# The scan of a two-block transformer: four units of the recurrence side by side in TensorE's array, token rows moved by DMA through scratch memory

## The reference, cut to what matters

```python
inv_n = 2.0 / (MB * Dh)
def step(W, kv):
    kc, vc = kv
    z = jnp.einsum('bhsd,bhde->bhse', kc, W)
    grad = jnp.einsum('bhsd,bhse->bhde', kc, (z - vc) * inv_n)
    return (W - LR * grad, z)
_, zs = lax.scan(step, W0, (k_c, v_c))
```

## Time and profile before

| | us |
|---|---|
| median of three runs | 1100.81 (1100.41 to 1100.90) |
| the profiled execution | 1098.78 |
| its span in the trace | 1097.0 |

### The profile page before, as it was taken

One profiled execution on the slowest core, in us unless ns is written; L12 is line 12 of the kernel. 1 busy time (PEld: TensorE's weight loads), 2 busy tenths in 40 slices (PEclk: granted clock), 3 DMA queues, 4 the chain that ended last, 5 costly groups with the idle time before them and its releaser, 6 DMA issues. The chain is left out here.

```text
span 1097.0 us, 15610 instructions
## 1 busy us (share of the span) xinstructions
PE 1019.1 (93%) x5736; PEld 850.5 (78%) x5736; DVE 733.8 (67%) x1657; ACT 380.9 (35%) x731; POOL 227.2 (21%) x284
## 2 busy tenths in 40 slices
PE   6899999999999999998699999888999887999997
PEld 5688888888888888887588888667777775877775
DVE  7766667666666676666569866577878775466456
ACT  4334333333434333333133222044455433421220
POOL 2222222222222221222110011132222224111011
PEclk9999999999999999999999999999999998999999
DMA  9300000000000000000130000030000000000000
GB/s 302 110 1 1 1 1 1 1 1 1 1 1 1 1 1 1 1 1 16 33 100 1 1 1 1 0 98 0 0 0 0 1 2 1 1 15 15 10 20 19
DMA packets 19058, 20.91 MB, mean 19 GB/s; under 512 B 4905, under 2 KB 14898, under 8 KB 18994
## 3 DMA queue, kind: packets, MB, share of 16 engines
q1 hardware_dynamic: 18994, 20.05, 5.6%
HBM read 17.95 MB, written 2.10 MB: 18 GB/s over the span
## 5 line engine op out<-in xcount | busy, mean ns | idle before, releaser
L393 POOL TENSOR_TENSOR rope_sum<-rope_cos,rope_sin 128x512 f32<-128x512 f32 x80 | 115.0, 1437 | 257.0 <-DVE rope_sin L514 257.0
L429 ACT ACTIVATE rope_exp<-rope_sum 128x512 f32<-128x512 f32 x80 | 50.5, 631 | 205.7 <-POOL rope_sum L393 205.6
L783 PE MATMUL proj<-wo_sb,attn_out_t 128*128 128x256 f32 x512 | 113.2, 379 | 0.7 <-issue 0.7
L783 PEld LDWEIGHTS proj<-wo_sb,attn_out_t 128*128 128x128 f32 x512 | 96.1, 190 | 13.4 <-issue 0.9
L732 PE MATMUL num<-v_ones,score_masked 128*128 128x129 f32 x512 | 100.2, 278 | 5.9 <-DVE score_masked L572 5.9
L1754 DVE SCALAR_TENSOR_TENSOR m_acc<-m_expert,gates,m_acc 128x256 f32<-128x256 f32 x128 | 61.9, 484 | 58.6 <-PE m_expert L1833 52.1
L733 PE MATMUL num<-state,q_t 128*128 128x129 f32 x512 | 99.9, 277 | 0.0
L732 PEld LDWEIGHTS num<-v_ones,score_masked 128*128 128x128 f32 x512 | 83.0, 193 | 13.4 <-DVE score_masked L572 8.0
L511 DVE TENSOR_TENSOR rope_cos<-proj,cos_sb 128x512 f32<-128x512 f32 x80 | 55.3, 691 | 52.6 <-PE proj L686 52.6
L1554 PE MATMUL g_ps<-t_u,k_rows 128*128 128x128 f32 x512 | 72.7, 284 | 17.2 <-DVE t_u L1403 16.4
L1554 PEld LDWEIGHTS g_ps<-t_u,k_rows 128*128 128x128 f32 x512 | 63.4, 191 | 31.0 <-DVE t_u L1403 27.8
(11 more groups left out here) (205 smaller groups left out, 1993.4 us busy)
## 6 DMA issues: line engine op xcount, KB each, us to landing
a_stage<-in_wqkv SPq DMA_DIRECT2D x6, 512.0 KB, 5.4
wo_sb<-in_wo SPq DMA_DIRECT2D x1, 2048.0 KB, 10.1
a_stage<-in_wgu SPq DMA_DIRECT2D x4, 512.0 KB, 9.2
out<-x_sb SPq DMA_DIRECT2D x16, 128.0 KB, 1.7
x_sb<-in_x SPq DMA_DIRECT2D x2, 768.0 KB, 11.5
f_wmod<-in_wmod SPq DMA_DIRECT2D x1, 1536.0 KB, 9.0
w_sb<-in_w SPq DMA_DIRECT2D x1, 1280.0 KB
a_wmod<-in_wmod SPq DMA_DIRECT2D x1, 1024.0 KB, 6.5
```

The lines of the kernel that those rows point to most:

```text
L393: pool.tensor_tensor(y[:, parity], t1[:, parity], t2[:, parity], ALU.add).then_inc(s["y_done"], 1)
L783: mm = pe.matmul(proj[:, b, 0:D], o_t[:, i, :], wo[:, i, :], start=(i == 0), stop=(i == H - 1))
```

## The change

**The scan's layout.** The four units share the array. For z each unit takes a window of 32 columns of k transposed (`k_turned`, of which 16 are of the minibatch) as weights, and writes to 32 partitions of its own of one bank: four matmuls, 32x128. For g each unit has 16 rows on partitions 32 j to 32 j + 15 of `kv_rows` and `u_rows` as weights and moving rows, and a PSUM bank of its own. u is one operation of 128x128 for all units, w one of 128x512. There is one chain in place of one for each batch.

**The rows.** k and v leave the tile layout (a token on a partition) by a DMA to scratch in device memory and come back in row layout, `kv_rows`; u goes the other way, and POOL then makes z as v - u (`keep_z`). All these DMAs are issued by SP.

**The rest.** `k_diag` and `k_rows` are gone, with ACT's work on them and their semaphores. The high part of h is made by ACT, the low part by POOL. Turning, normalising and writing out z happens one tile later (`c - 2` for `out_rows`). The loop over tiles is written out. In the mixture, the gates are padded with zeros from 9 to 128 columns, and b2 to 128 rows.

The diff, cut to its core:

```diff
+            UP = P // U
             xn, zn = self.t_xn, sb("t_zn", [P, B, D])
             h = sb("t_h", [P, B, KD, P])
...
-            k_diag = sb("k_diag", [P, B, KD, NMB * STEP])
-            k_rows = sb("k_rows", [P, B, NMB, D])
-            u = sb("t_u", [P, B, D])
-            w = sb("t_w", [P, B, KD, P])
+            kv = sb("t_kv", [P, 2, B, KD, 2, P])
+            k_t = sb("k_turned", [P, 2, U * P + MB])
+            kv_r, u_r = sb("kv_rows", [P, 2, NMB, 2, P]), sb("u_rows", [P, 2, NMB, P])
+            u_tok = sb("t_u", [P, B, D])
...
+            g_ps = ps("g_ps", [P, U, 512])
+            kv_dram = nc.dram_tensor("kv_scratch", (2, B, P, KD * 2 * P), F32, kind="Internal").ap()
...
-            def walk(engine, step):
-
-
-                step(0, False, True, True)
-                with nc.Fori(1, NC - 2, engines=(engine.engine,), hint_back_edge=True) as c:
-                    step(c, True, True, True)
...
+                def kv_rows(c, b):
+                    q = c % 2
+                    sp.wait_ge(kr_done, nth(b, c + 1))
+                    sp.wait_ge(v_kept, nth(b, c + 1))
+                    sp.dma_start(kv_dram[q, b], kv[:, q, b].rearrange("p k u e -> p (k u e)")).then_inc(kv_out[b], 16)
+                    if c >= 2:
+                        sp.wait_ge(g_full, 1 + (c - 1) * NMB)
+                        sp.wait_ge(u_done, (c - 1) * NMB)
+                    sp.wait_ge(kv_out[b], 16 * (c + 1))
+                    for k in range(KD):
+                        src = kv_dram[q, b].rearrange("(n s) (k d) -> k s n d", n=NMB, k=KD)[k]
+                        sp.dma_start(kv_r[unit(b, k), q].rearrange("s n u e -> s n (u e)"), src).then_inc(kv_in[b], 16)
+
+                def u_rows_out(c):
+                    q = c % 2
+                    sp.wait_ge(u_done, (c + 1) * NMB)
+                    for b in range(B):
+                        for k in range(KD):
+                            dst = u_dram[q, b].rearrange("(n s) (k d) -> k s n d", n=NMB, k=KD)[k]
+                            sp.dma_start(dst, u_r[unit(b, k), q]).then_inc(u_out[b], 16)
+                    for b in range(B):
+                        if c:
+                            sp.wait_ge(z_kept, nth(b, c))
+                        sp.wait_ge(u_out[b], 16 * KD * (c + 1))
+                        sp.dma_start(u_tok[:, b], u_dram[q, b]).then_inc(u_in[b], 16)
+
+                sp.wait_ge(zeroed, 1)
+                for b in range(B):
+                    kv_rows(0, b)
                 w2, b1, b2, gw = self.moe_small
...
+                pool.memset(kv_r[:], 0.0).then_inc(zeroed, 1)
+                pool.memset(k_t[:, :, U * P:U * P + MB], 0.0).then_inc(zeroed, 1)
+
+                def low(c, b):
+                    pool.wait_ge(hi_done, nth(b, c + 1))
+                    pool.tensor_tensor(h_lo[:, b], h[:, b], h_hi[:, b].bitcast(F32), ALU.subtract).then_inc(hl_done, 1)
+
+                def keep_z(c, b):
+                    pool.wait_ge(u_in[b], 16 * (c + 1))
+                    if c:
+                        pool.wait_ge(zn_done, nth(b, c))
...
-                def spread(c, b, j, waited=True):
-
-                    if waited:
-                        act.wait_ge(g_full, nth(b, c * NMB + (j - NMB + 2)))
-                    act.activation(k_rows[:, b, j], kr[:, b], ACT.Copy, scale=rows_of[:, j:j + 1]
-                                   ).then_inc(k_rows_done, 1)
...
+                def high(c, b):
+                    act.wait_ge(h_done, nth(b, c + 1))
+                    if c:
+                        act.wait_ge(proj_full, nth(b, c))
+                    act.activation(h_hi[:, b], h[:, b], ACT.Copy).then_inc(hi_done, 1)
...
+                def residual(c, n):
+                    i = c * NMB + n
+                    dve.wait_ge(z_full, i + 1)
+                    if n == 0:
+                        for b in range(B):
+                            dve.wait_ge(kv_in[b], 16 * KD * (c + 1))
+                            if c >= 2:
+                                dve.wait_ge(u_out[b], 16 * KD * (c - 1))
+                    dve.tensor_tensor(u_r[:, c % 2, n], kv_r[:, c % 2, n, 1], z_ps[:, 0:P], ALU.subtract).then_inc(u_done, 1)
+
+                def new_w(i):
+
+                    dve.wait_ge(g_full, i + 1)
+                    dve.tensor_tensor(w[:], g_ps[:, :, 0:P], blocks[:].unsqueeze(1).broadcast_to([P, U, P]), ALU.mult
+                                      ).then_inc(w_done, 1)
+
...
+                def values(c, n):
+
+                    pe.wait_ge(w_done, c * NMB + n + 1)
+                    if n == 0:
+                        pe.wait_ge(kt_done, nth(1, c + 1))
+                        if c == 0:
+                            pe.wait_ge(zeroed, 2)
+                    for j in range(U):
+                        col = j * P + n * MB
+                        mm = pe.matmul(z_ps[UP * j:UP * (j + 1), 0:P], k_t[:, c % 2, col:col + UP], w[:, j],
+                                       start=True, stop=True)
+                    mm.then_inc(z_full, 1)
+
+                def gradient(c, n):
+
+                    pe.wait_ge(u_done, c * NMB + n + 1)
+                    if n == 0:
+                        for b in range(B):
+                            pe.wait_ge(kv_in[b], 16 * KD * (c + 1))
+                    for j in range(U):
+                        rows = slice(UP * j, UP * j + MB)
+                        mm = pe.matmul(g_ps[:, j, 0:P], kv_r[rows, c % 2, n, 0], u_r[rows, c % 2, n],
...
+                    def beside_u(n):
+                        if n in (0, 1, 2) and nxt:
+                            project(c + 1, n // 2, (0, 2, 1)[n])
+                        if n in (3, 4) and c >= 2:
+                            out_rows(c - 2, n - 3, 0)
+                        if n == 5 and nxt:
+                            k_turn(c + 1, 0)
+                        if n == 5 and not nxt:
+                            self.turn_group(pe, 0, kv_ps)
+                        if n == 7 and ahead:
+                            norm_turn(c + 2)
+
+                    def beside_w(n):
+                        if n in (0, 1, 2) and nxt:
+                            project(c + 1, (n + 1) // 2, (1, 0, 2)[n])
+                        if n in (3, 4) and c >= 2:
+                            out_rows(c - 2, n - 3, 1)
+                        if n == 5 and nxt:
+                            k_turn(c + 1, 1)
+                        if n == 7 and prev:
...
-            gates = sb("gates", [P, 2, GT, E + 1])
-            gates_t = sb("gates_t", [E + 1, 2, GT, P])
+            gates = sb("gates", [P, 2, GT, P])
+            gates_t = sb("gates_t", [P, 2, GT, P])
...
-                    act.activation(gates_t[:, g % 2], small[0:E + 1, :].rearrange("p (i t) -> p i t", i=GT), ACT.Copy
+                    act.activation(gates_t[:, g % 2], small[:].rearrange("p (i t) -> p i t", i=GT), ACT.Copy
...
-                dve.memset(gates[:], 1.0)
+                dve.memset(gates[:], 0.0).then_inc(s["gate_step"], 1)
+                dve.wait_ge(s["gate_step"], 1)
+                dve.memset(gates[:, :, :, E:E + 1], 1.0)
...
-                        t = pe.transpose(small[0:E + 1, i * P:(i + 1) * P], gates[:, g % 2, i, :], ident[:])
+                        t = pe.transpose(small[:, i * P:(i + 1) * P], gates[:, g % 2, i, :], ident[:])
```

More of the change, by code:

```diff
@@ L1216, in _ @@
                 for b in range(B):
+                    low(0, b)
+                for b in range(B):
                     x_rstd_of(pool, b, 2)
                 for b in range(B):
[L1219 to L1231, removed]
+                    add_rope(0, b)
+                pool.memset(self.moe_small[2][:], 0.0).then_inc(zeroed, 1)
+                for b in range(B):
+                    low(1, b)
+                for c in range(NC):
+                    prev, nxt, ahead = c > 0, c + 1 < NC, c + 2 < NC
                     if ahead:
@@ new lines, in _ @@
+                    if prev:
+                        for b in range(B):
+                            z_rstd_of(c - 1, b)
+                    if c >= 2:
+                        for b in range(B):
+                            add_rows(c - 2, b)
+                    if ahead:
+                        for b in range(B):
+                            low(c + 2, b)
+                    if not nxt:
+                        for i in range(3):
+                            self.chunk_low(pool, NCH + i, i * WCH, min(WCH, NH * P - i * WCH))
@@ L1288, in _ @@
                 for b in range(B):
[L1289 to L1296, removed]
-                    for j in (2, 3):
+                    keep_v(0, b)
+                for b in range(B):
+                    keep_k(0, b)
@@ L1423, in step @@
[L1423 to L1432 removed]
+                        if n == 2 and nxt:
+                            rope_sin(c + 1, 0)
@@ L1495, in _ @@
                     mm.then_inc(g_full, 1)
-                for b in range(B):
-                    norm_turn(b, 1)
+                for j in range(U):
```

(11 more changed lines are left out.)

438 lines of the change are left out of this document (209 added, 229 removed).

## The result

The changed kernel takes 1129.8 us (1128.68 to 1131.15) against 1100.6 before: slower by 2.7%, ratio 1.0269 (1.0251 to 1.0287). The forecast was 1096, in a range of 1050 to 1130, and faster. The profiled execution's span grew from 1097.0 to 1127.6.

A forecast was written before the change was run, and what follows sets the result against it. The scan's bare step was taken as bound by one batch's chain, with side work on a full PE. Loop -12.8, start +7.1, end +7.0 and mixture -5.5 sum to -4.2 us, giving 1096, range 1050 to 1130.

The forecast's parts named there:

- the rival of the clock: Scan loop: granted clock may fall to its lower level, 1.07 us a step, 68 us, giving 1165; chance 0.08.
- The overlap of z and g: Scan step: a unit's two records follow each other, so eight streams become five; z 0.73 us, g 0.81.
- the rival's 0.41 and 0.48: Scan step: all four units at once, z 0.41 and g 0.48, 0.65 us a step less, giving 1054; chance 0.22.
- Loads of weights: Scan's g: a rival had weights load in turn, g staying at 1.16 us, 22 us more, 1118; chance 0.17.
- the last tile: Scan's last tile: the mixture's work on DVE inside the chain, and transposes beside u, add 4.2 us.
- Side work: Scan loop: hidden except beside u, where projection parts, Wo matmuls and transposes stick out; 4.3 to 10.9 us, taken as 8.
- The DMAs: Row transfers around the scan: each leg costs 0.46 us of issue and 1.7 to landing; only the ends lack cover.
- The start: Scan's start: u waits for both batches' rows, first u at 729.1 against 722.96, 6.1 us; slower clock about 1 more.
- the end: Scan's end: u's way out and back and POOL's z take 6.9 us, 6.5 more than before; 7.0 with a wait.
- the cover of 9 us: Middle of the scan: k's way out and back needs 4.8 us and has some 9, so no wait.
- The mixture: Mixture: padding removes two switches from each of 16 token tiles, 0.38 us each, 6.1 in all; taken as 5.5.
- steps of 2.70: Scan loop: a step without side work takes 2.70 us, 64 steps 172.8; named as a sign of a right forecast.

The follow-up runs named there:

- burn_head: The changed kernel with 45 extra unused matmuls on PE while it waits for the first rows of k and v: 1128.0 us, ratio 1.024.
- burn_light: burn_head plus unused matmuls in step gaps without side work, two beside u and three beside w: 1078.1 us, ratio 0.979.
- g_full: The changed kernel with g's matmuls over all 128 rows instead of the unit's 16 (result left wrong): 1112.7 us, ratio 1.0106.
- best: burn_light with both batches' k and v sent out before fetching, 30 start matmuls, and extra matmuls where PE waits long: 1069.0 us, ratio 0.9721.
- best2: best with 18 in place of 45 extra matmuls ahead of the last turning of z: 1068.2 us, ratio 0.9706.
- burn_heavy: burn_light with four extra matmuls beside w and one more behind side work beside w: 1085.0 us, ratio 0.981.

## Why the prediction was wrong

**The step that failed is the clock.** The forecast kept it at 1.00 through the loop and gave its fall 0.08, with the reason that before it fell only where PE stood still, while "here it works in each half of a step". That reason was wrong: PE worked in each half, as the windows show (busy for 183.7 of 210.7 us), and yet the clock stayed at 0.51. With a full clock at the start it went in the bare steps in the middle of the first tile, where PE has 0.42 and 0.50 us of records in 2.16 (`burn_head`). Keeping it was worth 59.6 us (`burn_light`), against 68 that the rival had. That 1129.8 still lies within the range of 1050 to 1130 is luck: the range left the rival of the clock out.

**The overlap of z and g** was forecast as pairs, 0.73 and 0.81. It is full: 0.42 and 0.50, the rival's 0.41 and 0.48. The objection to it, that the two records of a unit keep the others waiting, did not hold: the trace of `burn_head` has the four first records of z from 740.76 on, 7 ns apart, and the four second ones 0.13 us later, again 7 ns apart. "TensorE: Matmul & The Clock Gate", Part 3, in the Trainium skill reports concurrent starts about 4 ns apart for matmuls on different row groups; the trace agrees that g's start together, and has 7 ns. The 0.42 of z are 0.275 of a lone record, one stream of 0.107, and some 0.04 for the starts. Loads of weights do not queue: eight of g, of 0.18 us each, lie within 0.31.

**Both at once was not among the rivals.** Each was priced alone. The rival of the clock came to 1165, because it doubled ten streams. With full overlap 1054 is the base, and the low clock adds 0.24 and 0.31 a step to z and g (35 us); the side work and the last tile take 38.5 us (210.7 less 64 times 2.69) in place of 12.2 (+26), and the DMAs' two ends 7.5 more: 1123 of the 1129.8. Most of the rest is the chain: 2.69 less the 0.55 of the clock is 2.14 a step, where the rival's sum gives 2.05, so 6 us. Of the 26 us, 1.6 are not the clock: DVE's low part of h in the last tile takes 3.24 us in place of 1.63, and it does so in `burn_light` too; no run tells why. So some 24 us of the clock's cost lie in the side work and the last tile, beside the 35 in the scan's own matmuls. That the overlap itself is what empties PE, `g_full` bears out for g; for z it is argued.

**Side work** beside u was to cost 8 us in the loop at the full clock; a step with two parts of the projection takes 2.32 against 2.16 (`burn_head`). That is 0.16, where the forecast had 0.33 if PE must empty and 0.16 if it need not. So the switch costs little there, and the row of nine-row matmuls, 0.19 each, was the wrong one for it. At the lower clock it is 0.94 (3.63 against 2.69), because pieces of 1.22 us no longer fit their gaps.

**The DMAs** were mis-sized. A leg was 1.7 us to landing; measured are 2.0 out and 3.5 back for k and v (pieces of 1 KB and many rows), 2.3 out and 2.0 back for u. The start lost 9.9 us, not 6.1, and the end 10.7, not 7.0. Of these 3.7 more at the end, 1.4 are the way of u: z is kept 8.3 us after the last u (943.54), not 6.9. The rest lies behind it, where the batches are turned and multiplied together at the lower clock:

```profile
951.13 0.73 POOL L1248 TENSOR_TENSOR t_z<-t_kv,t_u 128x256 f32<-128x256 f32 x1 [0.55 <-DMA t_u<-u_scratch]
...
959.30 3.76 PE L1569 MATMUL t_turn<-t_wo,t_o 128*128 128x256 f32 x8 [1.59 <-ACT t_o L1337]
```

In `best`, at the full clock, the same eight records take 1.99 us. In the middle the cover of 9 us held at the slow pace; at the fast one the rows come up to 1.9 us late.

**The mixture** was right in its mechanism, 0.38 against 0.39 a token tile. In the changed kernel, where the clock was low for some 10 us at its start, it gained 5.1. Alone on the kernel before, padding gained 9 in all, with the clock no longer falling in three groups.

By the forecast's own points: first u near 729 (732.8), steps of 2.70 (2.69, at another clock), PEclk below 1 named as the mark of a wrong forecast.

## What to carry to other kernels

A change that makes PE's work denser in the array makes it shorter in time, and the rest of the chain stays. So ask for the clock whenever PE's records shrink against the step, and price a rival together with the one that brings it about. If the granted clock falls, try more work for PE before undoing the layout, and put it also where PE waits for a DMA: here unused matmuls in the gaps, with an earlier start of the DMAs, turned a loss of 2.7% into a gain of 2.9%. Look at several executions, since a loop that drops the clock once can go on at the lower one with the extra work on top. A row's landing time holds for its shape of transfer only: 128 KB back from memory in pieces took 3.5 us, a plain store of 128 KB 1.7.

## What the runs showed of the hardware

Four matmuls of 32 columns each or of 16 rows each ran fully side by side, eight records in 0.42 and 0.50 us at the full clock, and in 0.66 and 0.81 at half. The granted clock, 2.4 GHz at 1.00 and 1.2 at 0.50, stayed at the lower level for over 200 us with PE's records covering 87% of the loop. With unused work in the gaps from the start it stayed at 1.00 in the loop (`burn_light`, `best`, `best2`), and with g's 1.16 us in place of 0.50 it rose to 0.96. Lost in the middle of the loop of `burn_heavy`, it stayed at 0.50 though PE's records covered all of the time. Which property of the work the chip looks at was not tested.
